# Minima first, ACT and VectorE work respread, and stacks of q and k read back by six DMAs in a two-layer transformer kernel

## The chip, the core and the metric

The kernel runs on one NeuronCore of one Trainium2 chip. A core has TensorE (PE; matmuls, its weight loads shown as PEld), VectorE (DVE), ScalarE (ACT), GpSimd (POOL), SyncE (SP, which issues all DMAs here) and 16 DMA engines. The metric is the device time of one execution in microseconds (us), lower is better.

## What is computed

Sixteen sequences of 256 tokens and 256 features run through two layers; all arithmetic that matters is float32.

```python
# layer 0
tgt1 = _layer_norm(tgt, g1, be1)
tgt = tgt + _self_attn(tgt1, mask, Wq, bq, Wk, bk, Wv, bv, Wo, bo)
tgt = tgt + (memory @ Wg.T + bg)
tgt1 = _layer_norm(tgt, g2, be2)
ff = relu(tgt1 @ W1.T + b1) @ W2.T + b2
x = tgt + ff
# layer 1
x = layer_norm(targets, ln1_s, ln1_b)
x = mha(x, x, sa_wq, sa_wk, sa_wv, sa_wo, causal=True) + targets
y = layer_norm(x, ln2_s, ln2_b)
y = mha(y, encoded, ca_wq, ca_wk, ca_wv, ca_wo, causal=False) + x
z = layer_norm(y, ln3_s, ln3_b)
out = y + relu(z @ mlp_w1 + mlp_b1) @ mlp_w2 + mlp_b2
```

Attention has 16 heads of width 16. The layer 0 mask is data; `encoded` and `memory` are the same context.

## The kernel before, in words

**Passes and steps.** There are three passes over the 16 sequences: pass 0 (layer 0 with its MLP), pass 1 (causal self-attention of layer 1, no MLP), pass 2 (cross-attention and the MLP of layer 1). A task is one sequence in one pass, 48 in all. A step has 16 slots, h = 0 to 15, one for each head. In a step several tasks are at work at once: `nxt2` (layer norm, transposes), `nxt` (q, k and v projections, then the stacks), `cur` (scores of head h in slot h), `prev` (rest of attention, output projection) and `old` (MLP). Every engine runs its own `slot(st, h)` function for h = 0 to 15 and so has a fixed order; engines meet only through semaphores. A wait holds up everything behind it on that engine.

**q, k and the stacks.** To get float32 accuracy from bf16 matmuls, q and k are split into three bf16 parts each. ACT copies the projection from PSUM twice, as bf16 (`q_part[:, 0]`, slot 3; `k_part[:, 0]`, slot 4) and as float32 (`q_f`, `k_f`). GpSimd subtracts, VectorE casts the second part (slots 5 and 6), GpSimd makes the third. SP writes the parts to the DRAM tensor `parts` (lines 381 and 390, two DMAs each) and reads them back, stacked, into `q_stack` and `k_stack` (lines 399 and 404): six blocks of 16 partitions each, `Q_PARTS = (0, 0, 1, 1, 0, 2)` against `K_PARTS = (0, 1, 0, 1, 2, 0)`, so that one matmul over 96 rows sums the six products of parts. A block is one DMA: 16 partitions, in each of them two runs of 4 KB. The first scores of a step wait for all twelve (`stacked`). DRAM holds q and k as (m, d, h, s), with m the half of the heads.

**Scores and after.** In slot h TensorE computes the scores of head h into one of two PSUM banks (`s_ps`, line 494), after VectorE is done with head h - 2. VectorE's `score_guard` (line 858 in passes 0 and 1, 843 in pass 2) adds the bias and takes the minimum of each row (q has its sign turned). In pass 0 ACT takes the exponential (line 712), TensorE transposes (line 508), and ACT (even heads, 819) or VectorE (odd heads, 994) copies to `prob_t`. In passes 1 and 2 the minima of four heads are split in three bf16 parts by GpSimd (`top_part`), turned by TensorE into rows 96 to 107 of `o_ps` (line 521, 12 weight columns placed with `tile_position`), copied by ACT into rows 96 to 107 of `q_stack` (729), and TensorE computes the transposed scores with the minima already subtracted (542); ACT exponentiates (721). Then come the values (572), transposes and normalising of `o` on VectorE (885 to 926, from slot `NORM_AT` on), and the output projection.

**Other work in VectorE's slots.** In a slot the guard comes last. Ahead of it stand, by slot: casts of `h_hi` (slots 7 to 10), statistics of `nxt2` (slot 9), its mean (10, with `ve = variance + eps`), v out of PSUM (11), its normalising (12), the same for the MLP's layer norm (14, 15), and the result `y_sb` (15). `rstd` is a power on GpSimd. `affine` on ACT (line 736) reads a transposed tensor from PSUM and applies scale and shift twice, once rounded to the high part (`xt_hi`, `x2t_hi`) and once in float32 (`tf_a`, `tf_b`), two halves each.

## Time and profile before

| | us |
|---|---|
| median of 3 runs | 1724.61 |
| lowest, highest | 1707.62, 1731.74 |
| the profiled execution: its own time | 1704.09 |
| its span (first to last instruction) | 1702.3 |

| engine | busy us | share of the span |
|---|---|---|
| PE | 1459.5 | 86% |
| PEld | 1175.9 | 69% |
| DVE | 1212.1 | 71% |
| ACT | 1061.9 | 62% |
| POOL | 834.7 | 49% |

The mean granted TensorE clock is 0.956 of full speed. In the profile, times are microseconds unless marked ns; L494 is line 494 of the kernel. "Idle before" is the time an engine stood still before an instruction, put down to what ended it. The chain of waits follows the work that ended last back to what released it. DMA share is the mean busy share of the 16 DMA engines, and GB/s what they moved. Scores of pass 0's steady steps run from about 66 to 640 us, those of pass 1 from about 750 to 1190, those of pass 2 to about 1650.

### The profile page before, as it was taken

How to read it: one execution, taken by the hardware profiler on the slowest of the kernel's cores; microseconds unless marked ns; L12 is line 12 of the kernel's file. 1: busy time of each engine (PE TensorE's matmuls, PEld its weight loads, DVE VectorE, ACT ScalarE, POOL GpSimd, SP SyncE). 2: the span in 40 equal slices, each digit the busy share in tenths (PEclk: the TensorE clock that was granted, in tenths of full speed). 3: DMA queues.
4: the chain of work that ended last, by engine and by line, in shares of the span. 5: the costliest groups of instructions: out<-in, count | busy, mean ns of one | idle time of the engine just before them, and what ended most of it. 6: DMA issues, size and time to landing. Idle time of an engine off the chain costs nothing.

```text
span 1702.3 us, 42833 instructions
## 1 busy us (share of the span) xinstructions
PE 1459.5 (86%) x13376; PEld 1175.9 (69%) x13376; DVE 1212.1 (71%) x3855; ACT 1061.9 (62%) x2153; POOL 834.7 (49%) x1125
## 2 busy tenths in 40 slices
...
GB/s 145 139 113 119 108 109 118 99 99 105 117 100 99 105 125 130 119 107 107 124 121 111 129 101 140 115 153 93 119 112 105 99 128 99 105 101 129 79 26 13
DMA packets 163511, 185.75 MB, mean 109 GB/s; under 512 B 15952, under 2 KB 140240, under 8 KB 163408
## 3 DMA queue, kind: packets, MB, share of 16 engines
q1 hardware_dynamic: 163408, 184.57, 49.8%
...
HBM read 125.78 MB, written 58.72 MB: 108 GB/s over the span
## 4 chain that ended last, share of the span: by engine, by line
PE 42%; issue 13%; ACT 12%; DVE 12%; DMA 9%; POOL 6%; SPq 5%; ACTq 1%; DVEq 0%; POOLq 0%
PE d_ps L437 16%; PE d_ps L673 8%; DMA k_stack<-parts 7%; PE o_ps L572 5%; PE s_ps L494 5%; PE t_ps L542 3%; DVE prob L858 3%; PE t_ps L508 3%; SPq L399 2%; DMA parts<-q_part 2%; ACT prob_t L721 2%; SPq L404 2%; DVE o_n L890 2%; POOL h_lo L1031 2%; PE m_ps L444 1%
## 5 line engine op out<-in xcount | busy, mean ns | idle before, releaser
L721 ACT ACTIVATE prob_t<-t_ps 128x384 f32<-128x384 f32 (+1 forms) x512 | 275.4, 551 | 393.0 <-PE t_ps L542 197.7
L494 PE MATMUL s_ps<-k_stack,q_stack 96*128 96x256 bf16 (+1 forms) x1536 | 294.6, 275 | 124.5 <-DMA k_stack<-parts 47.5
L712 ACT ACTIVATE prob<-prob,neg_max 128x256 f32<-128x256 f32 x512 | 233.8, 514 | 121.0 <-DVE neg_max L858 118.8
L494 PEld LDWEIGHTS s_ps<-k_stack,q_stack 96*128 96x128 bf16 x1536 | 115.1, 100 | 227.8 <-issue 65.7
L542 PE MATMUL t_ps<-q_stack,k_stack 108*128 108x256 bf16 (+1 forms) x1024 | 207.3, 269 | 23.0 <-ACT prob_t L721 14.3
L858 DVE CUSTOM_DVE_ANT_0 prob<-s_ps,bias_sb 128x256 f32<-128x256 f32 x512 | 192.4, 416 | 48.5 <-PE s_ps L494 36.7
L858 DVE CUSTOM_DVE_ANT_0 prob<-s_ps,causal 128x128 f32<-128x128 f32 (+1 forms) x512 | 158.5, 352 | 90.2 <-PE s_ps L494 88.0
L843 DVE TENSOR_REDUCE top<-s_ps 128x2 f32<-128x512 f32 x256 | 172.9, 682 | 54.8 <-PE s_ps L494 51.3
L1031 POOL TENSOR_TENSOR h_lo<-h_f,h_hi 128x512 fp32r<-128x512 f32 x128 | 165.9, 1296 | 86.6 <-DVE h_hi L921 86.6
L572 PE MATMUL o_ps<-prob_t,v_sb 128*17 128x256 f32 (+1 forms) x3072 | 200.7, 381 | 0.0
L437 PE MATMUL d_ps<-x2t_hi,w_hi 128*128 128x256 f32 x512 | 157.0, 307 | 38.2 <-ACT k_f L780 21.8
L901 DVE STREAM_TRANSPOSE o_q<-o_ps 128x256 f32<-128x256 f32 x192 | 86.1, 449 | 133.0 <-PE o_ps L572 131.4
L508 PE MATMUL t_ps<-ident_sb,prob 128*128 128x128 f32 x1024 | 160.3, 280 | 2.5 <-DVE prob_t L994 2.0
L673 PE MATMUL d_ps<-w_hi,h_hi 128*128 128x256 f32 x512 | 148.0, 289 | 4.4 <-POOL h_lo L1031 4.4
L673 PE MATMUL d_ps<-w_hi,h_lo 128*128 128x256 f32 x512 | 147.5, 288 | 0.0
L673 PE MATMUL d_ps<-w_lo,h_hi 128*128 128x256 f32 x512 | 146.4, 286 | 0.1
L437 PE MATMUL d_ps<-x2t_lo,w_hi 128*128 128x256 f32 x512 | 145.7, 285 | 0.0
L437 PE MATMUL d_ps<-x2t_hi,w_lo 128*128 128x256 f32 x512 | 145.4, 284 | 0.0
L729 ACT ACTIVATE q_stack<-o_ps 12x1024 bf16<-12x1024 f32 x128 | 130.1, 1016 | 11.5 <-PE o_ps L521 6.7
L437 PEld LDWEIGHTS d_ps<-x2t_hi,w_hi 128*128 128x128 f32 x512 | 98.8, 193 | 52.4 <-issue 44.1
L508 PEld LDWEIGHTS t_ps<-ident_sb,prob 128*128 128x128 f32 x1024 | 121.8, 144 | 14.0 <-issue 6.6
L1031 POOL TENSOR_TENSOR x2t_lo<-tf_b,x2t_hi 128x512 fp32r<-128x512 f32 x32 | 40.9, 1277 | 181.8 <-ACT tf_b L736 181.8
...
## 6 DMA issues: line engine op xcount, KB each, us to landing
...
```

The costliest lines, as they stand in the source:

```text
L437: last = mm(dst, lhs, rhs, start=(opens and n == 0), stop=(closes and n == len(terms) - 1))
L494: last = mm(s_ps[:, h % 2, q * S:q * S + n], q_stack[0:ROWS, t.par, HEAD[h], q * P:(q + 1) * P], k_stack[0:ROWS, t.par, HEAD[h], 0:n], sta ...
L508: last = nc.tensor.transpose(t_ps[:, h % 2, c:c + P], prob[:, h % 4, q, k * P:(k + 1) * P], ident_sb[:, :])
L542: last = mm(t_ps[:, h % 2, k * S:k * S + S - lo], k_stack[:, t.par, HEAD[h], k * P:(k + 1) * P], q_stack[:, t.par, HEAD[h], lo:S], start=T ...
L572: last = mm(o_ps[32 * j:32 * j + VW, lo:S], v_sb[:, t.par, k, HEAD[h], :], prob_t[:, h % 8, k * S:k * S + S - lo], start=(k == 0), stop=(k ...
L673: last = mm(d_ps[:, 0, t * D:(t + 1) * D], lhs, rhs, start=(f == 0 and n == 0), stop=(f == FT - 1 and n == 2))
L712: last = nc.scalar.activation(prob[:, h % 4, q, :], prob[:, h % 4, q, :], ACT.Exp, bias=neg_max[:, h % 4, q:q + 1], scale=-1.0)
L721: nc.scalar.activation(prob_t[:, h % 8, 0:n], t_ps[:, h % 2, 0:n], ACT.Exp, scale=-1.0)\
L729: nc.scalar.activation(rows, o_ps[ROWS:ROWS + TOP, S:2 * S].unsqueeze(1).to_broadcast([TOP, CH, S]), ACT.Copy).then_inc(top_row.sem, 1)
L843: v.tensor_reduce(top[:, h // CH % 2, :, h % CH], s_ps[:, h % 2, :].rearrange("p (q k) -> p q k", q=TT), AX_X, ALU.min).then_inc(u_done.se ...
L858: last = v.tensor_tensor_reduce(prob[:, h % 4, q, 0:n], s_ps[:, h % 2, q * S:q * S + n], bias, 1.0, HUGE, ALU.add, ALU.min, least)
L1031: g.tensor_tensor(dst, a, b, ALU.subtract).then_inc(done, 1)
```

## The change

**Readback.** The projection weights' columns and `parts` are ordered (d, h, s), so that one d has all 16 heads in one run of 8 KB. The blocks are ordered by `RUNS = ((0, 3), (1, 2), (2, 1))`: q holds part 0 three times, part 1 twice, part 2 once; k holds beside them parts 0 to 2, parts 0 and 1, part 0. Each run is one DMA: for q with a repeated source (`to_broadcast`), for k from consecutive parts. The number of matmul rows and products is the same.

**Order and place of work.** On VectorE `score_guard` and the odd copy of `prob_t` come first in a slot instead of last. Statistics, mean and normalising of `nxt2` move from slots 9, 10, 12 to 4, 5, 6, the normalising of o in pass 0 from slot 6 to 7. `ve` is made by GpSimd. v of passes 1 and 2 is copied by ACT in one instruction instead of by VectorE in two. ACT reads each transposed or projected tensor from PSUM once, as float32, and makes the high part by a copy of that (`high_part`), with a semaphore of its own (`xt_h`, `x2t_h`, `ct_h`, `q_p1`, `k_p1`) for those that need it. The minima are turned with 108 weight columns, 96 of them zero, and no `tile_position`. The causal bias is one [128, 256] tile.

```diff
-Q_PARTS = (0, 0, 1, 1, 0, 2)
-K_PARTS = (0, 1, 0, 1, 2, 0)
-NBLK = len(Q_PARTS)
+RUNS = ((0, 3), (1, 2), (2, 1))
+NBLK = sum(n for _, n in RUNS)
...
-NORM_AT = (6, 10, 10)
+NORM_AT = (7, 10, 10)
+STATS_AT, MEAN_AT, HAT_AT = 4, 5, 6
...
-                    for j, part in enumerate(Q_PARTS):
-                        sp.dma_start(q_stack[j * HD:(j + 1) * HD, t.par].rearrange("d (m h) s -> d m (h s)", m=KC),
-                                     parts[t.par, 0, part].rearrange("m d h s -> d m (h s)")).then_inc(stacked.of(t), 16)
+                    row = 0
+                    for part, n in RUNS:
+                        sp.dma_start(q_stack[row:row + n * HD, t.par].rearrange("p h s -> p (h s)"),
+                                     parts[t.par, 0, part].rearrange("d h s -> d (h s)").unsqueeze(0)
+                                     .to_broadcast([n, HD, H * S])).then_inc(stacked.of(t), 16)
+                        row += n * HD
...
-                    for j, part in enumerate(K_PARTS):
-                        sp.dma_start(k_stack[j * HD:(j + 1) * HD, t.par].rearrange("d (m h) s -> d m (h s)", m=KC),
-                                     parts[t.par, 1, part].rearrange("m d h s -> d m (h s)")).then_inc(stacked.of(t), 16)
+                    row = 0
+                    for _, n in RUNS:
+                        sp.dma_start(k_stack[row:row + n * HD, t.par].rearrange("p h s -> p (h s)"),
+                                     parts[t.par, 1, 0:n].rearrange("j d h s -> (j d) (h s)"))\
+                            .then_inc(stacked.of(t), 16)
+                        row += n * HD
...
-                    last = mm(o_ps[ROWS:ROWS + TOP, S + q * P:S + (q + 1) * P],
-                              top_part[:, c % 2, q].rearrange("p j n -> p (j n)"), ident_bf[:, :],
-                              start=True, stop=True, tile_position=(0, ROWS))
+                    last = mm(o_ps[0:ROWS + TOP, S + q * P:S + (q + 1) * P], top_wide[:, c % 2, q, :], ident_bf[:, :],
+                              start=True, stop=True)
...
+            def high_part(task, dst, src, made, done):
+
+                act.wait_ge(made.sem, made.after(task))
+                act.sem_inc(passed, 1)
+                nc.scalar.activation(dst, src, ACT.Copy).then_inc(done.sem, 1)
...
-                    affine(x2t_hi, tf_b, c, c + 2, x2t_f)
+                    affine(tf_b, c, c + 2, x2t_f)
+                    high_part(st.old, x2t_hi[:, :, :], tf_b[:, :, :], x2t_f, x2t_h)
...
+                if h == V_AT + 1 and has(st.nxt, KEYED):
+                    act.wait_ge(v_mm.sem, v_mm.after(st.nxt))
+                    if st.prev:
+                        act.wait_ge(pv_mm.sem, pv_mm.after(st.prev))
+                    act.sem_inc(passed, 1)
+                    nc.scalar.activation(v_sb[:, st.nxt.par, :, :, 0:HD],
+                                         d_ps[:, 1, :].rearrange("p (k h d) -> p k h d", k=TT, d=HD), ACT.Copy)\
+                        .then_inc(v_done.sem, 1)
...
-                dve.wait_ge(mv_done.sem, mv_done.after(task))
-                v.tensor_scalar(ve_t[:, :], mv_t[:, :, 1], eps, None, ALU.add).then_inc(ve_done.sem, 1)
...
+                if has(st.cur):
+                    score_guard(st, h)
+                t, ht = head_at(st, h, LAG, (0,))
+                if t and ht % 2:
+                    dve.wait_ge(t_mm.sem, t_mm.after(t, ht + 1))
+                    ring_free(dve, st, t, ht)
+                    v.tensor_copy(prob_t[:, ht % 8], t_ps[:, 1, :]).then_inc(pt_odd.sem, 1)
...
-                if h == 10 and has(st.nxt2):
+                if h == MEAN_AT and has(st.nxt2):
+                    pool.wait_ge(ln_mv.sem, ln_mv.after(st.nxt2))
+                    pool.sem_inc(passed, 1)
+                    g.tensor_tensor(ve[:, :], mv[:, :, 1], eps_sb[:, st.nxt2.p], ALU.add).then_inc(ln_ve.sem, 1)
                     pool.wait_ge(ln_ve.sem, ln_ve.after(st.nxt2))
...
-    lanes = np.arange(D).reshape(KC, H // KC, HD).transpose(0, 2, 1).reshape(-1)
+    lanes = np.arange(D).reshape(H, HD).T.reshape(-1)
```

The order of SyncE's instructions in one step of pass 0, from the writes of the parts on, before (the counts behind a DMA are its destination's, `x5` is five alike):

```order
L381 DMA parts<-q_part 128x3x256 [waits stacked_0,q_p2,q_p3]
L381 DMA parts<-q_part 128x3x256
L390 DMA parts<-k_part 128x3x256 [waits k_p2,k_p3]
L390 DMA parts<-k_part 128x3x256
L396 REGISTER_ALU [waits s_mm]
L399 DMA q_stack<-parts 16x2x2048 [waits q_written_0]
L399 DMA q_stack<-parts 16x2x2048 x5
L404 DMA k_stack<-parts 16x2x2048 [waits k_written_0]
L404 DMA k_stack<-parts 16x2x2048 x5
```

and in a step of the change (passes 1 to 2, where `st_mm` stands in place of `s_mm`):

```order
L382 DMA parts<-q_part 128x3x256 [waits q_p2,q_p3]
L382 DMA parts<-q_part 128x3x256
L391 DMA parts<-k_part 128x3x256 [waits k_p2,k_p3]
L391 DMA parts<-k_part 128x3x256
...
L401 DMA q_stack<-parts 48x1x4096 [waits q_written_1]
L401 DMA q_stack<-parts 32x1x4096
L401 DMA q_stack<-parts 16x4096
L409 DMA k_stack<-parts 48x4096 [waits k_written_1]
L409 DMA k_stack<-parts 32x4096
L409 DMA k_stack<-parts 16x4096
```

Twelve reads into 16 partitions became six, into 48, 32 and 16 partitions, behind the same waits. As the instructions carry them, the source of the first has the counts 3, 16, 4096 with a step of 0 in the first, that of the second 2, 16, 4096.

VectorE in slots 9 to 11 of a step of pass 2, before (`top` are the minima of a head, `o_q`, `o_n`, `o_f` the attention output on its way):

```order
L864 BN_STATS stats<-x_in 128x6
L841 REGISTER_ALU
L843 TENSOR_REDUCE top<-s_ps 128x2 [waits s_mm]
L885 RECIPROCAL rden<-o_q 128x32 [waits o_done]
...
L890 TENSOR_TENSOR o_n<-o_q,rden 128x2x8x16
L920 REGISTER_ALU
L921 CAST h_hi<-h_f 128x512 [waits h_done]
L868 REGISTER_ALU [waits ln_rstd,x_hat]
L871 BN_AGGR mv<-stats 128x2 [waits ln_stats]
...
L874 TENSOR_SCALAR ve<-mv 128x2 [waits ln_mv]
L841 REGISTER_ALU
L843 TENSOR_REDUCE top<-s_ps 128x2 [waits s_mm]
```

and of the change:

```order
L865 TENSOR_REDUCE top<-s_ps 128x2 [waits s_mm]
L912 RECIPROCAL rden<-o_q 128x32 [waits o_done]
L913 REGISTER_ALU
L917 TENSOR_TENSOR o_n<-o_q,rden 128x2x8x16 [waits ot_f,rden_done]
L917 TENSOR_TENSOR o_n<-o_q,rden 128x2x8x16
L947 REGISTER_ALU
L948 CAST h_hi<-h_f 128x512 [waits h_done]
L863 REGISTER_ALU
L865 TENSOR_REDUCE top<-s_ps 128x2 [waits s_mm]
L933 STREAM_TRANSPOSE o_f<-o_n 128x512 [waits ot_l,o_norm]
```

The guard of slot 10 stood behind normalising, cast, mean and `ve`; of these the first two now follow slot 10's guard (shown first) and stand ahead of slot 11's, and the layer norm is in slots 4 to 6.

ACT in slots 3 and 4 of a step of pass 0, before (`prob` is the exponential of a head):

```order
L765 ACTIVATE q_part<-d_ps,cols_sb 128x256 [waits q_written_1,q_mm,q_p3]
L765 ACTIVATE q_part<-d_ps,cols_sb 128x256
L765 ACTIVATE q_f<-d_ps,cols_sb 128x256 x2
L290 REGISTER_ALU [waits t_mm]
L819 ACTIVATE prob_t<-t_ps 128x512 [waits pv_mm]
```

and of the change:

```order
L774 ACTIVATE q_f<-d_ps,cols_sb 128x256 [waits q_p3,q_mm]
L774 ACTIVATE q_f<-d_ps,cols_sb 128x256
L750 ACTIVATE q_part<-q_f 128x512 [waits q_written_1,q_done]
L291 REGISTER_ALU [waits t_mm]
L841 ACTIVATE prob_t<-t_ps 128x512 [waits pv_mm]
```

Four reads of PSUM became two and a copy of the float32 result; k (slot 4) has the same form.

## Rows read from the trace of the kernel before

**Rows 1.** stretches: length, busy us (count) PE, PEld, DVE, ACT, POOL, PEclk, DMA share, GB/s

```profile
212.32:635.00 422.68, 389.38 (x3550) 338.40 (x3549) 351.78 (x1145) 307.96 (x711) 207.67 (x173) 1.00 0.47 107
760.00:1190.00 430.00, 340.86 (x3404) 248.66 (x3404) 285.70 (x1221) 247.11 (x447) 184.12 (x367) 0.92 0.58 119
1240.83:1600.00 359.17, 337.73 (x3036) 267.54 (x3037) 258.48 (x514) 233.52 (x429) 206.50 (x317) 1.00 0.48 105
980.90:983.90 3.00, 2.97 (x30) 1.82 (x30) 1.44 (x8) 0.49 (x1) 0.11 (x1) 0.61 0.39 131
```

**Rows 2.** chain of waits, whole run: start us, us, what

```profile
751.77 2.35 DMA parts<-q_part
...
1157.44 2.36 DMA parts<-q_part
```

**Rows 3.** chain of waits, one step of pass 1

```profile
953.56 0.34 PE s_ps L494 x2
...
960.25 0.56 ACT k_part L783
...
964.00 0.38 SPq L381
...
966.88 0.32 SPq L399
...
971.92 8.88 DMA k_stack<-parts
...
980.93 0.34 PE s_ps L494 x2
...
992.85 0.37 SPq L381
```

**Rows 4.** SyncE timeline, pass 1: start us, us, engine line op out<-in xcount

```profile
1019.34 0.91 SPq L381 DMA_DIRECT2D parts<-q_part  x2
...
1043.82 0.90 SPq L381 DMA_DIRECT2D parts<-q_part  x2
```

**Rows 5.** stretches again (columns as rows 1): a load, and two stack readbacks

```profile
698.00:699.00 1.00, 1.00 (x13) 0.94 (x12) 0.07 (x1) 1.00 (x3) 0.00 (x0) 1.00 1.03 419
968.00:978.00 10.00, 8.32 (x86) 6.41 (x84) 8.53 (x41) 5.77 (x10) 2.87 (x6) 1.00 1.02 138
1329.00:1335.00 6.00, 6.00 (x59) 4.67 (x58) 3.89 (x12) 4.05 (x8) 3.10 (x4) 1.00 0.97 234
```

**Rows 6.** page, DMA packets of the run

```profile
DMA packets 163511, 185.75 MB, mean 109 GB/s; under 512 B 15952, under 2 KB 140240, under 8 KB 163408
```

**Rows 7.** VectorE timeline, slots 9 and 10 of a pass 2 step

```profile
1332.29 0.68 DVE L843 TENSOR_REDUCE top<-s_ps 128x2 f32<-128x512 f32 x1
...
1334.64 1.20 DVE L874 TENSOR_SCALAR ve<-mv 128x2 f32<-128x2 f32 x1
1335.76 0.68 DVE L843 TENSOR_REDUCE top<-s_ps 128x2 f32<-128x512 f32 x1
```

**Rows 8.** line 736: duration ns min/median/max, first and last start

```profile
L736 ACT ACTIVATE tf_b<-m_ps,cols_sb x64: 554/564/581, 114.3 to 1680.9; 128x256 f32<-128x256 f32 x64
```

**Rows 9.** TensorE's waits in four steps of pass 0: total us, times, longest

```profile
PE d_ps L437 <- ACT k_f L780: 6.7, 4, 1.7
PE s_ps L494 <- DVE neg_max L858: 3.9, 6, 0.8
```

**Rows 10.** SyncE and TensorE timelines, pass 0 then pass 2

```profile
322.64 2.66 SPq L399 DMA_DIRECT2D q_stack<-parts  x6
...
342.94 0.38 PE L494 MATMUL s_ps<-k_stack,q_stack 96*128 96x256 bf16 x2
...
1361.69 2.66 SPq L399 DMA_DIRECT2D q_stack<-parts  x6
...
1379.44 0.38 PE L494 MATMUL s_ps<-k_stack,q_stack 96*128 96x256 bf16 x2
```

**Rows 11.** page, costliest groups: weight loads of the scores

```profile
L494 PEld LDWEIGHTS s_ps<-k_stack,q_stack 96*128 96x128 bf16 x1536 | 115.1, 100 | 227.8 <-issue 65.7
```

More of the change, by code:

```diff
@@ L730, in top_copies, with affine @@
                                      ACT.Copy).then_inc(top_row.sem, 1)
-            def affine(high, dst, col_g, col_b, done):
-                for out_t in (high, dst):
-                    for k in range(KC):
-                        last = nc.scalar.activation(out_t[:, k, :], m_ps[:, k * S:(k + 1) * S], ACT.Identity,
-                                                    bias=cols_sb[:, col_b + k:col_b + k + 1],
-                                                    scale=cols_sb[:, col_g + k:col_g + k + 1])
+            def affine(dst, col_g, col_b, done):
+                for k in range(KC):
+                    last = nc.scalar.activation(dst[:, k, :], m_ps[:, k * S:(k + 1) * S], ACT.Identity,
+                                                bias=cols_sb[:, col_b + k:col_b + k + 1],
+                                                scale=cols_sb[:, col_g + k:col_g + k + 1])
                 last.then_inc(done.sem, 1)
+            def high_part(task, dst, src, made, done):
+                act.wait_ge(made.sem, made.after(task))
+                act.sem_inc(passed, 1)
+                nc.scalar.activation(dst, src, ACT.Copy).then_inc(done.sem, 1)
             def slot(st, h):
@@ L774, in slot @@
                         act.wait_ge(k_p3.sem, k_p3.after(st.cur))
[L775 to L785 removed]
+                    if st.nxt.p == 0:
+                        for m in range(KC):
+                            last = nc.scalar.activation(k_f[:, m, :], d_ps[:, 0, m * S:(m + 1) * S], ACT.Identity,
+                                                        bias=cols_sb[:, C_BK + m:C_BK + m + 1])
+                    else:
+                        last = nc.scalar.activation(k_f[:, :, :], d_ps[:, 0, :].rearrange("p (m s) -> p m s", m=KC),
+                                                    ACT.Copy)
+                    last.then_inc(k_done.sem, 1)
+                    if st.cur:
+                        act.wait_ge(k_written.of(st.cur), k_written.after(st.cur))
+                    high_part(st.nxt, k_part[:, 0], k_f[:, :, :], k_done, k_p1)
                 if h == 5 and has(st.prev, (0,)):
@@ L926, in slot @@
                     v.tensor_copy(ot_hi[:, :, :], o_f[:, :, :]).then_inc(ot_h.sem, 1)
-                if h == 9 and has(st.nxt2):
+                if h == STATS_AT and has(st.nxt2):
                     dve.wait_ge(x_landed.of(st.nxt2), x_landed.after(st.nxt2))
@@ L936, in slot @@
                         dve.wait_ge(ln_rstd.sem, ln_rstd.after(st.nxt))
-                    aggregate(st.nxt2, stats, mv, ve, LN_EPS[st.nxt2.p], ln_stats, ln_mv, ln_ve)
-                if h == V_AT + 1 and has(st.nxt):
+                    aggregate(st.nxt2, stats, mv, ln_stats, ln_mv)
+                if h == V_AT + 1 and has(st.nxt, (0,)):
                     dve.wait_ge(v_mm.sem, v_mm.after(st.nxt))
```

118 lines of the change are left out of this document (54 added, 64 removed).

## The prediction

> **What bounds the kernel now.** I read the three passes apart, because their steps differ. In passes 0 and 2 TensorE is busy 389.4 of 422.7 us and 337.7 of 359.2 us [rows 1]: it idles 33.3 us in the 11 steps of the first stretch (3.0 us each) and 21.4 us in about 10.6 steps of the second (2.0 us each). These passes are TensorE-bound, and an edit elsewhere can give back at most that idle time. Pass 1 has no MLP; there TensorE is busy only 340.9 of 430 us and its mean clock is 0.92 of full. The chain of waits says why. From the write of the q parts at 751.77 to that at 1157.44 lie 15 steps, 27.0 us each [rows 2], and one of them reads as a ring [rows 3]: first scores at 953.56, ACT's k_part after the key projection at 960.25, then GpSimd's k_f and the last q part, q parts write issued at 964.00, first stack read issued at 966.88, last one lands at 971.92 + 8.88 = 980.80, next scores at 980.93, next q parts write at 992.85. The ring of that step is 11.9 (scores to q write, 980.93 to 992.85) + 2.9 (to the first read) + 13.9 (reads) + 0.1 = 28.8 us. The step before took 10.4 instead of 11.9 us from scores to write; in the first 3 us after the wait of 980.9 the granted clock is 0.61, that is, TensorE falls to 1.2 GHz for much of it when it has idled [rows 1], and I charge 1.5 us for that. A step from 1019.34 to 1043.82 took 24.5 us [rows 4]; I take this as what pass 1 costs when the stacks come early.
>
> So in pass 1 the readback of the stacks is about half of the ring. What limits it? Not the issue: the last of 12 reads is issued at 971.92 and 8.9 us follow. The DMA engines are busy throughout (share 1.02) yet move 138 GB/s, and 234 GB/s in a good step of pass 2; a 1 MB load into 128 partitions reaches 419 GB/s, 26.2 per engine [rows 5]. Today each read fills 16 partitions from 16 rows, so that all 16 engines work on neighbouring partitions.
>
> **The change, part by part.**
>
> *Six reads in place of twelve.* The bytes stay 1.57 MB a step. Six issues fewer (2.66 us for six, [rows 10]) save nothing by themselves, since the transfer outlasts them. What counts is how the bytes fall on the engines. The k reads and the last q read are plain (48, 32 and 16 rows of 8 KB). The first two q reads have a repeat as their outermost source dimension: counts 3 x 16 x 8 KB and 2 x 16 x 8 KB, against 48 and 32 destination rows. In the kernel before, every outermost count is a multiple of 16, and the packets fit a spread over 16 engines each time: 15,952 packets under 512 B are 16 x 989 DMAs + 128 [rows 6]. No row shows what a count of 3 does. If a DMA is dealt to engines by the outermost entries that both sides share, these two go to 3 and to 2 engines. Then the first engine carries 128 + 128 + 8 KB of q and its sixteenth of k's 768 KB, 48 KB: 312 KB, where it carries 96 KB now. At 26.2 GB/s this takes 12.2 us; at the 14.6 GB/s per engine of the good pass 2 step (234/16), 21.9 us. The lone engines write far apart partitions, so they resemble the 419 GB/s row most; I take 25 GB/s, 12.8 us. Start and landing cost 13.9 - 1.57 MB / 138 GB/s = 2.5 us now. Reads: 15.3 us (ends 14.7 and 24.4), where they took 13.9 in the step shown.
>
> The Trainium skill speaks to this point (DMA: Bandwidth & Descriptors, "Why a DMA increments its semaphore by 16 and not by 1"): the engine count is the largest number up to 16 that divides the slowest non-unit dimension of both patterns, and its rules for kernel authors name a leading zero-stride broadcast as a trap. By it these two DMAs run on 3 and 2 engines; no run here shows it yet. The page SBUF — State Buffer ("Door 1") says 16 partitions reach 4 of 16 ports, about 109 GB/s as an estimate from its figures; the trace has more, 138 to 234, and the measurement decides. By that page alone, wider k reads would gain, which is the first rival below.
>
> *Minima first.* VectorE's guard of a head (L858, L843) moves ahead of the rest of its slot. In pass 2 the guard of slot 10 starts at 1335.76, 2.9 us after that of slot 9 ended at 1332.97, behind normalising, a cast and ve, which took 1.20 us [rows 7]; scores two heads on wait for it. *ACT.* An affine of four PSUM reads becomes two and one 512-wide copy. One such read is 0.564 us [rows 8] and a 512-wide one takes about as much (0.56, k_part in [rows 3]). So each of four such sites in a pass 0 step saves about one read, 0.5 us, and q_f and k_f come before their high parts instead of after, which frees the PSUM bank up to two reads, 1.1 us, sooner in pass 0. The waits they feed are TensorE's on k_f, 6.7 us in 4 steps of pass 0, and on the guard, 3.9 us [rows 9]: 2.65 us a step, most of its 3.0 us idle. In pass 1 this is off the ring, save that the copy now waits for k_f: +0.3 us before GpSimd's k_f. *v to ACT, ve to GpSimd, layer-norm to slots 4 to 6.* Same work elsewhere: VectorE is 66 to 83% busy over the three stretches, GpSimd 43 to 57%, ACT 57 to 73% [rows 1]. One v copy joins ACT and two leave VectorE. The normalise of slot 6 may now make VectorE wait for GpSimd's power behind two subtractions. The wider weights of the minima (108 columns for 12) are loads like those of the scores, 100 ns [rows 11], 256 times, beside running products: nothing, and at most 26 us over the run if none were hidden, which the 389 busy us beside it exclude. Of the possible 3.0 and 2.0 us I take 1.3 (pass 0) and 1.1 (pass 2), since other engines are close behind (VectorE is busy 83% in pass 0): 16 x 1.3 + 16 x 1.1 = -38 us; ends -80 and, by the third rival, 0 to +38.
>
> *Passes 0 and 2 and the slower reads.* First read at 322.64, next scores 342.94; 1361.69 and 1379.44 [rows 10]. With 15.3 us the stacks land 5.0 and 2.4 us early: hidden. Cover ends at 20.3 and 17.7 us of reads (less what the steps shrink).
>
> *Sum.* Pass 1's new ring: 11.9 + 2.9 + 15.3 + 0.1 + 0.3 = 30.5 us, against 27.0: +3.5. Of the readbacks, 16 feed pass 1's steps and one the first of pass 2: 17 x 3.5 = +60. 1704.1 (own time of the profiled execution) + 60 - 38 = 1726. The median of the runs shown is 1.2% above that execution; so 1746 to compare with 1724.6.
>
> **The rivals.**
> - *The q reads spread over 16 engines like the others.* For it: the destination has 48 rows, and no row of before contradicts it. Then every engine carries 96 KB and a DMA spans 32 or 48 partitions; at between 234 and 419 GB/s the reads take 3.8 to 6.7 us + 2.5, some 8 us, the ring drops to 23 us and pass 1 runs at its 24.5 us or a little below: -2.5 x 17 - 38 = -80, with minima-first perhaps -95. Time 1640. Chance 0.24; I see no way to cut a source of 3 repeats by 16 without re-deriving the pattern, hence not more.
> - *Lone engines are slow* (ends slower). If one engine alone stays nearer to 14.6 GB/s, or is held up by the 13 others' k rows, the reads take up to 24.4 us: ring 39.6 us, +12.6 x 17 = +214; passes 0 and 2 lose 24.4 - 20.3 = 4.1 and 6.7 us a step, +173. Up to 2053, on the scale of the medians 2078. It decides (over +2%, 34 us) once 17 x (ring - 27.0) exceeds 72 us: reads above 16.0 us, an engine below 23.7 GB/s. That is close to my value, so it has 0.25.
> - *The spreading costs rather than gives.* In pass 0 the first h_hi now stands behind guard, normalise of o and the moved layer-norm, VectorE being 83% busy, and ACT's h_f waits for the h_lo of two before. If each of 32 steps loses as much as ve did behind GpSimd, 1.2 us [rows 7], in place of the gain: 1726 + 38 + 38 = 1802, on the scale of the medians 1824. Against: slots 9 to 12 get lighter. 0.08.
>
> **How the numbers follow.** My forecast has 0.43: about 1746, own range 1700 to 1760. The first rival is faster by over 2% (about what a measurement of this kernel can tell from no change). Beside it, 0.06 of the forecast's chance lies below 1690, should minima-first give its full 80 us. Faster 0.30; slower: 0.25 + 0.08; same 0.37. The range from 1640 to 1825 leaves out half of the first rival and the worst of the second.
>
> **What would show it.** After: the first two q reads landing 6 to 12 us after issue while k's first parts wait for the first engines; DMA share during the reads well under 1 with GB/s falling after about 5 us; pass 1 steps near 30.5 us; a longer wait of TensorE on the stacks. If share stays at 1 and the stacks land within 9 us, the spread rival holds. For the rest: passes 0 and 2 at 38.1 and 32.9 us a step, k_f waits gone, the slot 10 guard right behind the slot 9 one. Wrong if pass 0's step grows, or if VectorE shows a wait on rstd in slot 6 that delays later guards.

## The result

| kernel | median us | ratio to before, 95% interval |
|---|---|---|
| before (beside this run) | 1720.15 | 1 |
| after | 2040.27 (2034.18 to 2044.78, 4 runs) | 1.186 (1.177 to 1.196) |

The change makes the kernel 19% slower, by 320 us. The forecast was 1746 us, 21 us above before, and its range ended at 1825 us: it was wrong in size, and its term for the order of the work (-38 us) was wrong in sign.

The step of a pass is read here as in [rows 2, 4], from one write of the q parts to the next, as a mean (us) from the 5th to the 15th write of the run for pass 0, the 20th to the 35th for pass 1, the 37th to the 47th for pass 2:

| step of | before | after | forecast |
|---|---|---|---|
| pass 0 | 39.4 | 44.5 | 38.1 |
| pass 1 | 27.0 | 38.2 | 30.5 |
| pass 2 | 34.0 | 38.0 | 32.9 |

(44.5 - 39.4) x 16 + (38.2 - 27.0) x 17 + (38.0 - 34.0) x 15 = 332 us, of the 338 us between the two profiled executions. All three passes lose, and by different mechanisms: pass 0 by the order of the work, pass 1 mainly by the late stacks, pass 2 by both, as e1 and e2 below separate them.

The page of the kernel after: busy time, the TensorE clock in 40 slices, DMA packets, and TensorE's costliest group, which waits for the stacks.

```profile
PE 1544.6 (76%) x13376; PEld 1261.3 (62%) x13376; DVE 1187.9 (58%) x3711; ACT 1055.5 (52%) x2073; POOL 851.4 (42%) x1209
PEclk7799898998989889888878877777799989998988
DMA packets 148390, 185.72 MB, mean 91 GB/s; under 512 B 10048, under 2 KB 134336, under 8 KB 139072
L501 PE MATMUL s_ps<-k_stack,q_stack 96*128 96x256 bf16 (+1 forms) x1536 | 309.9, 287 | 276.0 <-DMA k_stack<-parts 219.2
```

TensorE has as many instructions as before and is busy 85 us longer; its clock is at 7 to 9 tenths throughout, 0.869 in the mean for 0.956 before. Stretches of the three passes (length, busy us and count of PE, PEld, DVE, ACT, POOL, granted clock, DMA share, GB/s), to set beside [rows 1]:

```profile
340.00:640.00 300.00, 263.57 (x2238) 228.50 (x2238) 210.64 (x701) 188.08 (x421) 130.78 (x123) 0.93 0.34 93
930.00:1160.00 230.00, 135.68 (x1354) 102.53 (x1354) 108.64 (x504) 96.10 (x174) 72.45 (x149) 0.82 0.34 83
1500.00:1800.00 300.00, 263.01 (x2286) 212.71 (x2285) 195.96 (x357) 174.50 (x311) 160.02 (x256) 0.94 0.39 97
```

**The stacks.** SyncE's timeline and TensorE's first scores of one pass 1 step, answering to [rows 3]:

```profile
1120.14 0.91 SPq L382 DMA_DIRECT2D parts<-q_part  x2
1123.57 1.90 SPq L401 DMA_DIRECT2D q_stack<-parts  x3
1158.06 0.90 SPq L382 DMA_DIRECT2D parts<-q_part  x2
```

```profile
1145.09 0.50 PE L501 MATMUL s_ps<-k_stack,q_stack 96*128 96x128 bf16 x2 [9.43 <-DMA k_stack<-parts]
```

From the first read to the scores pass 21.5 us in this step; the forecast had 15.3 to the last landing, and the step of before in [rows 3] 13.9. That step of before was one of the slow ones: over 12 steady steps of pass 1 the time from the first read to the scores is 12.5 us in the mean before (10.4 to 14.3) and 21.2 after (20.8 to 21.6). The rest of the ring is 3.4 us from the write to the first read and 13.0 us from the scores to the next write.

**The engines' order.** TensorE's timeline in pass 0 (in brackets the idle time before, and what ended it), and stretches around two of its gaps:

```profile
471.38 0.39 PE L444 MATMUL d_ps<-w_hi,xt_hi 128*128 128x256 f32 x1 [2.38 <-ACT h_f L817]
491.41 0.65 PE L451 MATMUL m_ps<-ident_sb,x_hat 128*128 128x128 f32 x4 [1.07 <-DVE x_hat L898]
494.02 0.61 PE L501 MATMUL s_ps<-k_stack,q_stack 96*128 96x256 bf16 x2 [1.95 <-DVE neg_max L880]
```

```profile
468.00:471.00 3.00, 1.00 (x10) 0.73 (x7) 3.00 (x12) 2.13 (x6) 2.07 (x3) 1.00 1.05 167
471.40:474.40 3.00, 3.00 (x20) 2.89 (x21) 2.58 (x5) 2.00 (x5) 2.64 (x3) 0.76 0.92 227
490.00:494.00 4.00, 0.99 (x8) 0.52 (x5) 2.70 (x8) 0.21 (x2) 0.81 (x1) 0.93 0.20 68
494.00:497.00 3.00, 2.90 (x13) 2.45 (x14) 2.88 (x11) 3.00 (x7) 0.00 (x0) 0.50 0.86 254
```

After the second pair of gaps TensorE runs 3 us at half clock (0.50 granted, 1.2 GHz), after the first at 0.76. Before, the clock of pass 0 was 1.00 [rows 1]. So a gap costs its own length and then time at the lower clock. That VectorE waits for scores is new as well: its waits in 300 us of pass 0 (340 to 640 us; total us, times, longest), before, with the guard first alone (e6 below) and after:

```profile
DVE prob L858 <- PE s_ps L494: 10.9, 9, 1.3
DVE prob L858 <- PE s_ps L494: 76.5, 50, 3.1
DVE prob L880 <- PE s_ps L501: 79.2, 56, 3.7
```

### The profile page after: what moved, and what is told of

Same layout as the page of the kernel before. It is cut to its first block and busy times, and to the rows that moved or that the text cites. A ratio compares the mean times of both kernels' runs of the same rounds, so it can differ in the third digit from the quotient of the medians.

```text
span 2040.1 us, 42564 instructions
## 1 busy us (share of the span) xinstructions
PE 1544.6 (76%) x13376; PEld 1261.3 (62%) x13376; DVE 1187.9 (58%) x3711; ACT 1055.5 (52%) x2073; POOL 851.4 (42%) x1209
## 2 busy tenths in 40 slices
DMA packets 148390, 185.72 MB, mean 91 GB/s; under 512 B 10048, under 2 KB 134336, under 8 KB 139072
## 5 line engine op out<-in xcount | busy, mean ns | idle before, releaser
L727 ACT ACTIVATE prob_t<-t_ps 128x384 f32<-128x384 f32 (+1 forms) x512 | 268.9, 541 | 520.6 <-PE t_ps L552 295.6
L501 PE MATMUL s_ps<-k_stack,q_stack 96*128 96x256 bf16 (+1 forms) x1536 | 309.9, 287 | 276.0 <-DMA k_stack<-parts 219.2
L718 ACT ACTIVATE prob<-prob,neg_max 128x256 f32<-128x256 f32 x512 | 229.2, 501 | 149.8 <-DVE neg_max L880 149.5
L865 DVE TENSOR_REDUCE top<-s_ps 128x2 f32<-128x512 f32 x256 | 174.5, 685 | 213.9 <-PE s_ps L501 213.6
L548 PE MATMUL t_ps<-q_stack,k_stack 108*128 108x256 bf16 (+1 forms) x1024 | 220.6, 283 | 19.0 <-ACT q_stack L735 14.5
L578 PE MATMUL o_ps<-prob_t,v_sb 128*17 128x256 f32 (+1 forms) x3072 | 213.5, 401 | 0.0
L515 PE MATMUL t_ps<-ident_sb,prob 128*128 128x128 f32 x1024 | 167.7, 289 | 7.6 <-DVE prob_t L909 5.7
L679 PE MATMUL d_ps<-w_hi,h_hi 128*128 128x256 f32 x512 | 154.2, 301 | 5.0 <-POOL h_lo L1051 5.0
L817 ACT ACTIVATE h_f<-d_ps,cols_sb 128x256 f32<-128x256 f32 x256 | 107.1, 472 | 84.6 <-POOL h_lo L1051 77.3
L515 PEld LDWEIGHTS t_ps<-ident_sb,prob 128*128 128x128 f32 x1024 | 129.5, 150 | 19.8 <-issue 15.2
L1064 POOL TENSOR_TENSOR top_wide<-top,zeros 128x8 bf16<-128x8 f32 x128 | 31.2, 244 | 237.3 <-DVE top L880 205.7
```

Of the source, the lines that this page charges most:

```text
L501: last = mm(s_ps[:, h % 2, q * S:q * S + n], q_stack[0:ROWS, t.par, HEAD[h], q * P:(q + 1) * P], k_stack[0:ROWS, t.par, HEAD[h], 0:n], sta ...
L515: last = nc.tensor.transpose(t_ps[:, h % 2, c:c + P], prob[:, h % 4, q, k * P:(k + 1) * P], ident_sb[:, :])
L548: last = mm(t_ps[:, h % 2, k * S:k * S + S - lo], k_stack[:, t.par, HEAD[h], k * P:(k + 1) * P], q_stack[:, t.par, HEAD[h], lo:S], start=T ...
L578: last = mm(o_ps[32 * j:32 * j + VW, lo:S], v_sb[:, t.par, k, HEAD[h], :], prob_t[:, h % 8, k * S:k * S + S - lo], start=(k == 0), stop=(k ...
L679: last = mm(d_ps[:, 0, t * D:(t + 1) * D], lhs, rhs, start=(f == 0 and n == 0), stop=(f == FT - 1 and n == 2))
L718: last = nc.scalar.activation(prob[:, h % 4, q, :], prob[:, h % 4, q, :], ACT.Exp, bias=neg_max[:, h % 4, q:q + 1], scale=-1.0)
```

## The experiments

Each is compared with the kernel before on the same chip. Steps in us are means as above. "Interleaved" is explained at e3.

| kernel | ratio (95%) | median | pass 0 | pass 1 | pass 2 |
|---|---|---|---|---|---|
| before | 1 | 1714 to 1720 | 39.4 | 27.0 | 34.0 |
| after | 1.186 (1.177 to 1.196) | 2040 | 44.5 | 38.2 | 38.0 |
| e1 reads alone | 1.127 (1.124 to 1.130) | 1934 | 39.4 | 37.0 | 37.7 |
| e2 order alone | 1.079 (1.076 to 1.081) | 1851 | 44.4 | 29.0 | 36.8 |
| e3 after, interleaved | 1.070 (1.067 to 1.073) | 1834 | 44.3 | 28.2 | 36.8 |
| e4 after, twelve reads of 8 KB rows | 1.090 (1.087 to 1.093) | 1872 | 44.1 | 30.7 | 37.1 |
| e5 before, interleaved | 0.980 (0.976 to 0.984) | 1680 | 39.2 | 25.5 | 34.0 |
| e6 before, guard first | 1.065 (1.060 to 1.069) | 1825 | 44.4 | 29.2 | 35.1 |
| e7 = e3, guard last | 1.013 (1.009 to 1.017) | 1738 | 41.3 | 26.6 | 34.5 |
| e8 = e3, layer norm late | 1.016 (1.012 to 1.021) | 1743 | 41.1 | 27.3 | 34.6 |
| e9 = e3, both | 0.960 (0.957 to 0.964) | 1647 | 38.6 | 25.6 | 32.6 |
| e10 = e9, `NORM_AT` of pass 0 = 6 | 0.965 (0.961 to 0.969) | 1653 | 39.0 | 25.6 | 32.6 |
| e11 = e1, one leading repeat | 1.050 (1.046 to 1.054) | 1802 | 39.2 | 32.6 | 34.0 |
| e12 = e1, k read first | 1.145 (1.141 to 1.150) | 1966 | 39.5 | 37.7 | 39.2 |
| e13 = e9, guard first outside 7 to 10 | 1.003 (1.000 to 1.006) | 1722 | 40.9 | 27.3 | 33.8 |
| e14 = e9, guard first in 7 to 10 | 0.971 (0.965 to 0.976) | 1663 | 39.0 | 25.3 | 33.4 |
| e15 = e7, normalising late | 0.984 (0.979 to 0.990) | 1688 | 39.1 | 27.2 | 33.3 |
| e16 = e1, k reads small | one run | 1821 | 39.2 | 33.9 | 34.0 |
| e17 = e9, guard first in 5, 6 | 0.970 (0.964 to 0.975) | 1666 | 39.1 | 26.3 | 32.6 |
| e18 = e9, guard first in 11 to 15 | 0.979 (0.974 to 0.985) | 1682 | 40.4 | 25.6 | 33.2 |

### The two halves of the change: e1 and e2

e1 is the kernel before with the change's layout and its `RUNS` reads; e2 is the kernel after with them undone, the k reads for example, against after:

```diff
-                    row = 0
-                    for _, n in RUNS:
-                        sp.dma_start(k_stack[row:row + n * HD, t.par].rearrange("p h s -> p (h s)"),
...
+                    for j, part in enumerate(K_PARTS):
+                        sp.dma_start(k_stack[j * HD:(j + 1) * HD, t.par].rearrange("d (m h) s -> d m (h s)", m=KC),
...
```

> The kernel before with the six reads alone (and the layout that they need); order and place of the other work as before. Theory A (the two q reads with a leading repeat lie on 3 and 2 DMA engines, and that makes the stacks late): as slow as the full change or a little slower, 2040 to 2080 us, pass 1 steps near 40 us. Rival C (the respreading of VectorE's and ACT's work costs the time): near 1750 us, as forecast for the reads alone.

> The full change with its readback undone: the twelve reads of 16 partitions and two 4 KB rows as before, minima first and respread work as in the change. Theory A: 1680 to 1720 us (the forecast's own term, -38 us), pass 1 steps 27 us. Rival C: 1760 us or more.

e1 took 1934 us, e2 1851 us. Theory A alone and rival C alone both fall: each half costs, +220 and +137 us beside 1714. The reads cost pass 1 10.0 us a step and pass 2 3.7, pass 0 nothing; the order of the work costs 5.0, 2.0 and 2.8. The same 15 steps of pass 1, before and in e1:

```profile
751.35:1157.02 405.67, 321.31 (x3266) 235.70 (x3266) 271.60 (x1212) 231.99 (x421) 173.63 (x347) 0.92 0.59 121
779.15:1334.07 554.92, 336.66 (x3266) 243.57 (x3266) 272.68 (x1212) 231.99 (x421) 173.59 (x347) 0.81 0.36 89
```

From the first read to the scores e1 takes 21.3 us in the mean, 8.8 more than before; the same matmuls take 15.4 us more in the 15 steps at a granted clock of 0.81, 1.0 a step. Together these are 9.8 of the 10.0. In pass 2 both halves together cost 4.0, hardly more than the reads alone: with the order of the change (e2) 19.2 us pass there from the first read to the scores where before has 17.8, so more of a late readback is covered.

### The reads: e3, e4, e5

e3 keeps six reads of the same bytes and interleaves the rows of a run in both stacks, which the product over 96 rows allows, so that the repeat stands behind the 16 rows:

```diff
-                                     parts[t.par, 0, part].rearrange("d h s -> d (h s)").unsqueeze(0)
-                                     .to_broadcast([n, HD, H * S])).then_inc(stacked.of(t), 16)
+                                     parts[t.par, 0, part].rearrange("d h s -> d (h s)").unsqueeze(1)
+                                     .to_broadcast([HD, n, H * S])).then_inc(stacked.of(t), 16)
...
-                                     parts[t.par, 1, 0:n].rearrange("j d h s -> (j d) (h s)"))\
+                                     parts[t.par, 1, 0:n].rearrange("j d h s -> d j (h s)"))\
```

> The full change with the rows of a run interleaved: row d*n+j in place of j*16+d in both stacks, so that the repeat of q stands behind the 16 rows in the source (counts 16, n, 8 KB). Same six reads, same bytes, same 8 KB rows. Theory A: the reads spread over 16 engines, packets of 4 bytes rise from 9921 to 11216, stacks land 7 to 14 us after the first issue, 1600 to 1700 us. Rival B (8 KB rows into 48 and 32 partitions are slow on any engine): reads still near 20 us, 2000 us or more.

> The full change with twelve reads of 16 rows of 8 KB each (q part 0 three times, part 1 twice, part 2; k parts 0 to 2, 0 and 1, 0), blocks in the change's order. Theory A: 16 engines, reads 13 to 14 us as in the kernel before (ring 27 us), 1680 to 1720 us, like the readback of before. Rival B: 8 KB rows cost more than two 4 KB rows, reads near 20 us, 1900 us or more. If wider reads are what helps, this one is slower than the interleaved one.

> The kernel before with the six reads and interleaved rows alone (no guard first, no respreading). What e1 and e2 showed: the change's two halves cost 4.6 us (pass 0), 1.7 (pass 1) and 3.1 (pass 2) a step for the order and place of work, and 10 us a pass 1 step for the reads. If the reads spread over 16 engines hold here too, passes 0 and 2 stay at 39.4 and 34.0 us a step and pass 1 goes from 27.0 to 25 or 26: 1680 to 1700 us. If interleaved reads merely equal the twelve, 1714.

With the order of the change e3 takes 206 us less than after, though it is far above the 1600 to 1700 expected, because of the order's own cost. e5, the same reads in the kernel before, takes 1680 us, 2% below before. Its page, its chain of waits in a pass 1 step, and a stretch of its reads:

```profile
DMA packets 149686, 185.72 MB, mean 111 GB/s; under 512 B 11344, under 2 KB 135632, under 8 KB 140368
```

```profile
1055.22 0.56 SPq L399
...
1058.38 8.69 DMA k_stack<-parts
1067.13 0.34 PE s_ps L499 x2
```

```profile
1056.00:1066.00 10.00, 8.72 (x83) 6.89 (x82) 8.91 (x40) 5.48 (x10) 5.85 (x7) 0.92 0.98 184
```

The packets settle how the DMAs are dealt. Before has 15952 small packets, 16 for each of 989 DMAs and 128 more. The change issues 6 x 48 = 288 fewer, 701, and 701 x 16 + 128 = 11344, as here. After has 10048, that is 1296 fewer, and 48 x (13 + 14) = 1296: its two leading repeats run on 3 and on 2 engines. e11, where one repeat leads, the one of 3, has 10720, which is 48 x 13 fewer than 11344. By the rule of the Trainium skill quoted in the prediction (DMA: Bandwidth & Descriptors, "Why a DMA increments its semaphore by 16 and not by 1") they run on 3 and 2 engines as well: the trace agrees.

Spread over 16 engines the reads of this step take 11.9 us (1055.22 to 1067.13), at 184 GB/s; the slow step of [rows 3] had 138. In the mean over 12 steps it is 11.6 us (11.3 to 11.9) for 12.5 before, so 0.9 less, while the step is 1.6 us shorter; 0.4 us of that is the same matmuls at a clock of 0.94 for 0.92 (315.4 us busy in the 15 steps for 321.3), and the rest isn't traced. e4, whose twelve reads go to 16 partitions each, needs 2.5 us more a pass 1 step than e3. But it is also 1.7 us slower than e2, which has twelve reads into 16 partitions with two rows of 4 KB each in place of one of 8 KB. So six wider reads gain 2.5 us against twelve with the same 8 KB rows and 0.8 us (28.2 for 29.0) against the readback of before; the number of reads and their width aren't separated.

### What a leading repeat costs: e11, e12, e16

e11 keeps the leading repeat in the run of 3 alone; e12 issues k's reads ahead of q's; e16 leaves out 15 of the 16 heads of k: it cuts the k reads to `[..., 0:1, :]`.

> The kernel before with the six reads, rows j*16+d with the leading repeat in the run of 3 alone, the run of 2 interleaved. Theory A: the first engines carry 128 + 16 + 8 + 48 = 200 KB in place of 312 KB, so the reads end about 5 to 6 us before those of e1: pass 1 steps near 31.5 us in place of 37.0, 1780 to 1830 us. If the stacks are late for another reason than the bytes of the busiest engine (any leading repeat is bad in itself), close to e1, 1900 us or more.

> e1 (the kernel before with the six reads alone) with the three k reads issued ahead of the three q reads. The bytes on every engine stay, 312 KB on the first. Theory F (a lone engine moves some 26 GB/s when the others are still, and 13 GB/s while all of them read parts, so the order decides): k takes some 5 us on 16 engines and q then 264 KB at 26 GB/s, 10.2 us; reads 15 to 16 us in place of 18.7, pass 1 steps near 34.5 us, 1870 to 1900 us. Rival G (an engine that reads for a leading repeat has one rate, 312 KB in 18.7 us, 17 GB/s): as e1, 1934 us.

> e1 with its three k reads cut to one head, 512 bytes a row in place of 8 KB (the other heads of k_stack stay zero, so scores are computed on wrong k; the work is the same, and a memset and a wait at the start are added). The first engine still carries 264 KB of q. Theory H (the other 13 engines' k rows hold the lone engines up): 26 GB/s from the start, 10.3 us + 2.5, pass 1 steps 29 to 30 us, 1760 us. Rival I (engines that read the same rows for one repeat hold each other up, whatever else runs): 16 GB/s, 16.5 us + 2.5, pass 1 steps 34 to 35 us, 1880 us or more.

e11: 1802 us, in the range expected from the bytes of the busiest engine (200 KB for 312); 112 KB less take 4.4 us off, where 5 to 6 were expected (first read to scores 16.9 us in the mean for 21.3), which is 26 GB/s. e12: 1966 us, 32 above e1; theory F falls. Its readback takes 20.6 us in the mean, 0.7 less than in e1, but all of its reads wait for the write of k (first read 4.3 us behind the write of q, 1123.63 to 1127.97, for 2.9 in e1). Stretches of one readback of e1 (reads issued from 1114.68, next scores 1135.72), of e16 (1102.14 to 1120.19), and of the end of one of e12, where q's reads come last (next scores 1148.69):

```profile
1118.00:1122.00 4.00, 2.79 (x31) 1.85 (x32) 3.96 (x18) 0.49 (x1) 2.18 (x5) 0.88 1.04 197
1122.00:1127.00 5.00, 4.06 (x30) 3.29 (x27) 2.15 (x11) 4.20 (x8) 0.91 (x1) 0.75 0.19 51
1132.00:1134.00 2.00, 0.00 (x0) 0.00 (x0) 0.00 (x0) 0.00 (x0) 0.00 (x0) 0.50 0.13 52
1134.00:1137.00 3.00, 1.28 (x10) 0.79 (x14) 0.59 (x4) 0.22 (x1) 0.00 (x0) 0.50 0.07 27
```

```profile
1106.00:1113.00 7.00, 4.88 (x54) 3.62 (x52) 5.56 (x28) 4.06 (x8) 2.23 (x6) 1.00 0.19 56
1118.00:1121.00 3.00, 0.81 (x6) 0.65 (x6) 0.11 (x1) 0.00 (x0) 0.00 (x0) 0.50 0.06 24
```

```profile
1144.00:1148.00 4.00, 0.00 (x0) 0.00 (x0) 0.00 (x0) 0.00 (x0) 0.00 (x0) 0.50 0.13 52
```

The share times 16 gives the engines at work. With all 16, an engine moves 197 / 16 = 12 GB/s; with three (share 0.19), 51 / 3 = 17; with two (0.13), 26; the last one alone, 24 to 27. In e16, where almost no k is read, three engines still move only 56 / 3 = 19 GB/s each. So theory H falls, and rival I holds for the repeat of three: leaving k out takes 3.3 us off (21.3 to 18.0 in the mean), of which its own 48 KB at 25 GB/s are 2. (Its 1880 us were too high, since passes 0 and 2 hide 18 us.) As a rule for engines that read the same rows it doesn't hold: in e1 the repeat of two puts 112 KB more on the busiest engines than in e11, and these move at 26 GB/s; and in e12, if an engine serves its reads in the order of issue, the last 4 us are that repeat (128 KB an engine, and only 8 KB behind it), with 26 GB/s for each of its two engines, as much as one alone. What holds back three isn't shown; together they move 51 to 56 GB/s, two 52. Nor is it separated what the loads of the next step cost (`x_in` and `x_res`, issued at 1127.78 and 1128.53 in e1), during which all 16 engines are busy again for some 2 us.

### The order of work: e6 to e10, e15

e6 moves `score_guard` and the odd copy first in the kernel before, and nothing else; e7 moves them back last in e3; e8 (guard first) and e9 (guard last) change the line below, e15 (guard last) sets it to 4, 5, 12:

```diff
-STATS_AT, MEAN_AT, HAT_AT = 4, 5, 6
+STATS_AT, MEAN_AT, HAT_AT = 9, 10, 12
```

> The kernel before with one edit: guard and odd prob_t copy first in VectorE's slot. Theory D (the guard in front makes the cast h_hi, and so GpSimd's h_lo and ACT's next h_f, wait for the scores of the slot): passes 0 and 2 go from 39.4 and 34.0 to 43 and 37 us a step, 1820 to 1850 us. Rival E (the early layer norm or the copies of float32 results cost it): within 15 us of before, or faster.

> The full change with interleaved rows and with the guard and the odd copy last in the slot again. Theory D: 1690 to 1730 us, pass 0 near 39.5 us a step. Rival E: above 1790 us, close to the 1834 of the kernel with interleaved rows.

> The full change with interleaved rows and with the layer norm of nxt2 back in slots 9, 10, 12 (guard still first). Theory D: 1820 to 1850 us, little moved. Rival E with the layer norm as its cause (VectorE's slots 4 to 6 too full, GpSimd's k_f behind ve): 1700 to 1760 us.

Each of the two edits costs by itself: theory D holds for e6 and nearly for e7 (1738 us, expected up to 1730), but e8 moved as rival E expected of the layer norm. Against e3 the guard last gives back 96 us, the late layer norm 91, both (e9) 187: they add up. In e6, where the guard first alone costs 110 us, the chain is seen in one step of pass 0. VectorE, GpSimd, ACT and TensorE timelines:

```profile
432.91 0.42 DVE L858 CUSTOM_DVE_ANT_0 prob<-s_ps,bias_sb 128x256 f32<-128x256 f32 x1 [2.31 <-PE s_ps L494]
...
434.58 0.76 DVE L897 TENSOR_TENSOR o_n<-o_q,rden 128x256 f32<-128x256 f32 x2
435.26 0.42 DVE L924 CAST k_part<-k_f 128x512 bf16<-128x512 f32 x1
```

```profile
430.71 1.16 POOL L1031 TENSOR_TENSOR k_f<-k_f,k_part 128x512 f32<-128x512 f32 x1 [1.58 <-ACT k_f L780]
...
435.76 1.17 POOL L1031 TENSOR_TENSOR k_part<-k_f,k_part 128x512 bf16<-128x512 f32 x1 [2.76 <-DVE k_part L924]
436.88 1.57 POOL L1031 TENSOR_TENSOR ct_hl<-tf_b,ct_hl 128x512 fp32r<-128x512 f32 x1
438.41 1.46 POOL L1031 TENSOR_TENSOR h_lo<-h_f,h_hi 128x512 fp32r<-128x512 f32 x1
```

```profile
439.98 0.84 ACT L805 ACTIVATE h_f<-d_ps,cols_sb 128x256 f32<-128x256 f32 x2 [2.67 <-POOL h_lo L1031]
...
442.85 0.84 ACT L805 ACTIVATE h_f<-d_ps,cols_sb 128x256 f32<-128x256 f32 x2 [1.24 <-POOL h_lo L1031]
```

```profile
443.74 0.38 PE L437 MATMUL d_ps<-w_hi,xt_hi 128*128 128x256 f32 x1 [2.64 <-ACT h_f L805]
```

k_f is ready at 431.9, but its cast stands behind a guard that waits 2.3 us for scores, and behind the odd copy and the normalising of o, which follow the guard; GpSimd makes k_part, ct_lo (in `ct_hl`) and then h_lo late. ACT's h_f waits for that h_lo, the next h_f for the next h_lo (442.85), and TensorE for this second h_f. In the next 3 us the granted clock is 0.71. A stretch of e6's pass 0 has it at 0.92:

```profile
340.00:630.00 290.00, 251.89 (x2128) 220.23 (x2127) 210.49 (x694) 185.46 (x433) 129.30 (x109) 0.92 0.47 98
```

Per step of 44.4 us that is 38.6 us busy and 5.8 idle, where before, by [rows 1] and 39.4 us a step, it was 36.3 and 3.1: of the 5.0 us lost, 2.7 are new idle time and 2.3 the same work at a lower clock.

The early layer norm is seen in the chain of waits of after, pass 2: slot 6's normalising (L898) waits for ve and rstd on GpSimd, and a guard (L865) stands behind it, on which the next scores wait.

```profile
1429.29 0.54 DVE q_part L941
...
1431.01 0.38 POOL ve L1115
1431.46 0.70 POOL rstd L1119
1432.19 1.55 DVE x_in L898 x2
1433.74 0.61 DVE top L865
1434.40 0.62 PE s_ps L501 x2
```

> e7 (1738 us: guard last, layer norm of nxt2 in slots 4 to 6) with the normalising alone back in slot 12. The early layer norm costs 91 us between e9 and e7. If the normalising in slot 6 with its wait for rstd (1.1 us of work, 0.9 us of wait) pushes k_part, h_hi and h_f, most comes back: 1650 to 1680 us. If GpSimd's wait for the mean in slot 5 (8 us of standing still a step) or the statistics in slot 4 do it, 1710 us or more.

> The full change with interleaved rows, guard last and the layer norm of nxt2 back in slots 9, 10, 12; the ACT copies, v on ACT, ve on GpSimd, the wide minima and the normalising of o in slot 7 of pass 0 stay. e7 (guard last alone) has 41.2 us and e8 (layer norm late alone) 41.0 us a step in pass 0, the kernel before 39.4. If the two edits were all that costs, pass 0 falls to 39.4 or, should the forecast's gain of the shorter ACT work exist, to 38.1: 1650 to 1685 us. If one of the remaining edits costs, it stays at 40 us or above: 1700 us or more.

> As e9, with the normalising of o back in slot 6 of pass 0. If that edit costs in pass 0 (its cast ot_hi stands ahead of h_hi's neighbours in slot 8 in place of 7), up to 1 us a pass 0 step less than e9, some 15 us; else the same as e9 within 5 us.

e15 (1688) lies 50 us below e7 and 41 above e9: the normalising of slot 6 is a little over half of the layer norm's cost, statistics and mean the rest. So the expected "most comes back" was too much. e9 takes 1647 us, 4% below before, and 33 us below e5: what is left of the respreading (one PSUM read and a copy on ACT, v on ACT, ve on GpSimd, the wide minima, o normalised in slot 7) does gain, by 0.6 us a step in pass 0 and 1.4 in pass 2; which of these edits gains isn't separated, but for the slot of o: e10 is 7 us above e9, so slot 7 is a little better than slot 6. The page of e9:

```profile
PE 1416.2 (86%) x13376; PEld 1171.5 (71%) x13376; DVE 1175.0 (72%) x3711; ACT 1059.4 (64%) x2073; POOL 843.8 (51%) x1209
PEclk8799999999999999999999999998999999999999
```

### Which slots: e13, e14, e17, e18

In e9, guard and odd copy go first in some slots alone, for example the guard in e14:

```diff
+                if has(st.cur) and (7 <= h <= 10):
+                    score_guard(st, h)
...
-                if has(st.cur):
+                if has(st.cur) and (not 7 <= h <= 10):
                     score_guard(st, h)
```

> e9 (1647 us: interleaved rows, guard last, layer norm late) with guard and odd copy first in slots 0 to 6 and 11 to 15, and last in slots 7 to 10 alone, where the casts h_hi stand. Theory D (the guard ahead of h_hi is what costs): passes 0 and 2 stay at 38.6 and 32.6 us a step, 1640 to 1660 us. Rival J (a guard first costs in any slot, since VectorE then waits for the scores of the slot with work behind it): near e8, 1743 us, or in proportion of the slots, 1700 to 1720 us.

> e9 with guard and odd copy first in slots 7 to 10 alone. Theory D: close to e8, 1720 to 1745 us, TensorE waiting for ACT's h_f. Rival J: 1660 to 1680 us.

> e9 with guard and odd copy first in slots 5 and 6 alone, where the casts of the second parts of q and k stand. e6 showed VectorE waiting 2.3 us for the scores of slot 6 with the cast k_part behind it, then GpSimd's k_part and h_lo late. Theory K (these two slots carry the 75 us of e13): 1690 to 1720 us, pass 0 at 40.5 us a step. Rival L (the cost of e13 lies in slots 11 to 15, where the guard now stands ahead of x2_hat, which TensorE waits for in slot 1): 1645 to 1665 us.

> e9 with guard and odd copy first in slots 11 to 15 alone. Rival L: most of e13's 75 us, 1695 to 1725 us, TensorE waiting 1.2 us for x_hat and 1.8 us for the guard of slot 0 with a granted clock of 0.5 behind it, as in e13. Theory K: 1645 to 1665 us.

Theory D, on h_hi in slots 7 to 10, falls: these slots cost 16 us, the others 75. Slots 5 and 6 alone cost 20, 11 to 15 alone 35, so neither K nor L is the whole. 16 + 20 + 35 = 71 of the 96 us; slots 0 to 4 alone weren't tried, and some 20 us are left for them if the groups add up (75 - 20 - 35). Rival J fits e14 (1663 us, expected 1660 to 1680) and nearly e13 (1722, expected 1700 to 1720). TensorE's gaps in e13, pass 0, behind slot 15, and the stretches around them:

```profile
437.77 0.65 PE L451 MATMUL m_ps<-ident_sb,x_hat 128*128 128x128 f32 x4 [1.20 <-DVE x_hat L898]
440.25 0.49 PE L501 MATMUL s_ps<-k_stack,q_stack 96*128 96x256 bf16 x2 [1.82 <-DVE neg_max L880]
```

```profile
436.00:440.00 4.00, 1.22 (x10) 0.75 (x8) 2.83 (x6) 0.58 (x2) 1.17 (x1) 1.00 0.17 60
440.00:443.00 3.00, 2.55 (x12) 2.21 (x13) 3.00 (x13) 2.78 (x7) 0.00 (x0) 0.57 0.79 223
```

A guard in front waits for the scores of its own slot, with the work of other tasks behind it; it costs in every group of slots that was tried.

## Why the prediction was wrong, point by point

1. **What bounds the kernel**: right. Pass 1's ring has the readback in it, and 0.9 us off its mean (e5) gave 1.6 us a step there and 2% in all.
2. **How the two repeated reads are dealt**: right, 3 and 2 engines by the packets. The 138 to 234 GB/s that it set beside the estimate for one read into 16 partitions are of up to twelve such reads in flight, into 96 partitions, and don't test that estimate.
3. **The rate of a lone engine**: the step that failed in the first term. I took 25 GB/s for 312 KB because lone engines "resemble the 419 GB/s row most", hence 15.3 us of reads; measured 21.5 us in the step shown, 21.2 in the mean. With the 2.5 us of start and landing taken off, 312 KB in 19.0 us are 17 GB/s. 24 to 27 GB/s an engine has only when one or two are left; the repeat of three moves at 17 to 19, and at 12 while all 16 work. Even my own boundary (23.7 GB/s) lay above the truth, and the row nearest in kind, 16 engines reading this tensor at 234 / 16 = 14.6 GB/s, lay nearer. The term was +60 us; e1 has +220: 10.0 x 17 = 170 in pass 1 and 3.7 x 15 = 56 in pass 2. The sum had a second flaw: it took the parts of one slow step, whose ring is 28.8 us, and set the new ring against the mean of 27.0, so 1.8 of the +3.5 us a step were there before the change.
4. **Pass 2 and pass 0 hide the reads**: the covers of 20.3 and 17.7 us were right. e1's reads of some 21 us cost nothing in pass 0 and 3.7 us a step in pass 2; e11 and e16, with 33 and 34 us steps in pass 1, stay at 34.0 in pass 2.
5. **Minima first and the respreading, -38 us**: the second failed step, and its sign was wrong: +137 (e2). I priced the guard first as a gain from one place [rows 7], where it stood behind 1.2 us of work (and 2.8 us, not 2.9, behind the end of the guard before), and did not ask what would stand behind the guard: casts and layer norm that feed GpSimd, ACT and TensorE, while VectorE waits for scores (79.2 us in 300 us of after, 10.9 before, 76.5 with the guard first alone). That edit alone costs 110 us (e6). The rest of the respreading without the early layer norm comes to about the -38 us: e9 is 33 us below e5. That is partly luck, since the -38 was to come from the guard too, and by pass it is 0.6 and 1.4 us for 1.3 and 1.1.
6. **The bound on a loss**: 0 to +38. I took TensorE's idle time a step as what is at stake, but an edit can add idle time, and a gap lowers the clock: in e6 that made 2.3 of the 5.0 us a step. I charged the clock in pass 1 alone.
7. **The rivals**: rival 2 (lone engines slow, 0.25) and rival 3 (respreading costs, 0.08) both came true. Rival 3 named the mechanism, h_hi behind the guard and ACT's h_f behind h_lo, but priced it at 1.2 us a step, where e2 has 5.0 in pass 0 and 2.8 in pass 2. I weighed them as cases that exclude each other, though they concern different engines; with both, the range had to reach beyond either.
8. **What would show it**: the share fell (0.34 for 0.58), and the stacks' wait grew to 219.2 us from 47.5. TensorE's waits for k_f in 300 us of pass 0 fell as forecast, 11.7 to 2.3 us, but those for h_f rose from 4.4 to 18.7. Both signs named as "wrong if" came: pass 0's step grew to 44.5 us, and VectorE waiting for rstd in slot 6 ahead of a guard is the chain shown above.
